# Cross-attention with a token branch on one core: unit maxima two or three a step, score halves issued singly, tile scores spread over the weighting phases

## The reference

```python
query = x @ Wq;  keyt = enc @ Wk;  valt = enc @ Wv      # enc: the first 150 context rows
hs = mha(query, keyt, valt)                             # 8 heads of 80, softmax over 150 keys
ca_q1 = einsum('btc,th->bch', ca, Wq_ca)                # 384 rows of rank 4
ca_q1 = ca_q1[:, linspace(0, 383, 2048), :]             # 384 rows repeated to 2048
ca_hs1 = mha(ca_q1, x, x)                               # softmax over the 2048 rows of x
ca_hs2 = mha(ca_hs1 @ Wq, ca @ Wk_ca, ca @ Wv_ca)       # softmax over 4 tokens
out = (hs + ca_hs2) @ Wout + b_out + x
```

## Time and profile before

| | |
|---|---|
| time of three runs | 1560.33, 1560.63, 1563.39 us; median 1560.63 |
| the profiled execution | 1563.7 us, of which the span is 1561.6 us |
| granted TensorE clock, mean | 0.994 |
| busy share PE, PEld, DVE, ACT | 97%, 80%, 51%, 40% |
| weighting phases of the batches, first exponential of the first phase to that of the second | 34.1, 33.2, 34.2, 33.1 us |
| second phase, to the end of its last exponential | 26.7 us in each batch |
| from there to the split of tile 1's output (ACT, line 1090) | 22.2 us in each batch |

### The profile page before, as it was taken

The page is one execution under the profiler, slowest core; times in us unless marked ns, Lnnn a source line. Parts: engine busy times, 40 slices in busy tenths (PEclk is TensorE's granted clock), DMA queues, the critical chain, the costliest instruction groups (busy, mean ns, idle before and its releaser), DMA issues.

```text
span 1561.6 us, 24534 instructions
## 1 busy us (share of the span) xinstructions
PE 1511.6 (97%) x10294; PEld 1245.7 (80%) x10294; DVE 791.3 (51%) x1595; ACT 617.7 (40%) x1310; POOL 2.8 (0%) x12
## 2 busy tenths in 40 slices
PE   5999999999999999999999999999999999999998
PEld 4763599999976379999997438999998744999998
DVE  5786335343467443543447826344345872443533
ACT  1427724233243853323333484223323367332322
POOL 0000000000000000000000000000000000000000
PEclk9999999999999999999999999999999999999999
DMA  6630012130253001122025200114004510021101
GB/s 233 212 131 33 1 38 84 49 118 26 93 173 118 1 6 57 65 86 77 35 105 184 86 1 20 55 53 154 18 34 154 176 37 1 19 93 57 60 18 42
DMA packets 46679, 117.26 MB, mean 75 GB/s; under 512 B 3661, under 2 KB 5317, under 8 KB 45019
## 3 DMA queue, kind: packets, MB, share of 16 engines
q1 hardware_dynamic: 37036, 93.91, 17.3%
q10 hardware_dynamic: 9535, 21.80, 3.6%
HBM read 77.33 MB, written 39.17 MB: 75 GB/s over the span
## 4 chain that ended last, share of the span: by engine, by line
PE 85%; DVE 7%; ACT 5%; issue 3%; DMA 0%; SPq 0%; ACTq 0%
PE ps_w L502 43%; PE ps_s L502 17%; PE ps_t L502 15%; PE ps_t L512 5%; DVE unit_max L1290 4%; ACT work L1107 4%; PE ps_w L512 3%; PE ps_s L512 1%; ACT work L1077 1%; ACT ot L1021 0%; DMA y_all<-in_L_xattn_Wv_ca_dram 0%; DVE xt_l L1375 0%; DVE neg_max L1344 0%; DVE ot L1405 0%; ACT ot L1090 0%
## 5 line engine op out<-in xcount | busy, mean ns | idle before, releaser
L502 PE MATMUL ps_w<-wo_h,ot 128*128 128x320 f32 x1280 | 310.4, 314 | 0.6 <-DVE ot L1405 0.6
L1290 DVE TENSOR_REDUCE unit_max<-ps_s 128x1 f32<-128x512 f32 x384 | 240.1, 684 | 51.3 <-PE ps_s L502 50.2
L1077 ACT ACTIVATE work<-ps_s,neg_max 128x150 f32<-128x150 f32 x512 | 155.6, 409 | 211.7 <-DVE neg_max L1348 211.7
L502 PEld LDWEIGHTS ps_w<-wo_h,ot 128*128 128x128 f32 x1280 | 220.3, 188 | 0.9 <-DVE ot L1405 0.9
L502 PE MATMUL ps_w<-wo_l,ot 128*128 128x320 f32 x640 | 197.4, 308 | 0.0
L502 PE MATMUL ps_w<-v_all,work 120*128 120x162 f32 (+1 forms) x1280 | 171.3, 288 | 1.9 <-ACT work L1072 1.9
L502 PEld LDWEIGHTS ps_w<-v_all,work 120*128 120x128 f32 x1280 | 170.3, 190 | 3.4 <-ACT work L1072 2.9
L502 PE MATMUL ps_s<-keys_h,qt_h 128*128 128x300 f32 (+1 forms) x448 | 138.1, 308 | 0.0
L502 PE MATMUL ps_s<-keys_h,qt_l 128*128 128x300 f32 (+1 forms) x448 | 131.5, 294 | 0.0
L502 PE MATMUL ps_s<-keys_l,qt_h 128*128 128x300 f32 (+1 forms) x448 | 131.0, 292 | 0.0
L1416 DVE TENSOR_TENSOR work<-ps_w,xc 128x320 f32<-128x320 f32 x128 | 62.5, 489 | 133.6 <-PE ps_w L502 133.6
(11 more groups left out here) (163 smaller groups left out, 2258.1 us busy)
## 6 DMA issues: line engine op xcount, KB each, us to landing
xc<-in_x_dram SPq DMA_DIRECT2D x32, 1280.0 KB, 6.6
out_dram<-work ACTq DMA_DIRECT2D x64, 320.0 KB, 2.2
xt_all<-work SPq DMA_DIRECT2D x60, 256.0 KB, 2.5
xt_l<-xt_all SPq DMA_DIRECT2D x12, 1280.0 KB, 5.6
y_all<-in_L_xattn_Wk_dram SPq DMA_DIRECT2D x4, 960.0 KB
y_all<-in_L_xattn_Wv_dram SPq DMA_DIRECT2D x4, 960.0 KB
pick<-pick_all SPq DMA_DIRECT2D x16, 194.0 KB
xc<-in_L_xattn_Wq_dram SPq DMA_DIRECT2D x1, 1600.0 KB, 10.7
```

The source lines that it names most:

```text
L502: return nc.tensor.matmul(out, lhs, rhs, start=start, stop=stop, skip_group_check=True)
L1077: return nc.scalar.activation(probs[:, h * KEYS:(h + 1) * KEYS], ps_s[:, bank, c * KEYS:(c + 1) * KEYS], exp, bias=neg_max[:, s % 2, h:h + ...
L1290: v.tensor_reduce(unit_max[:, a, n, q:q + 1], bank, AX_X, ALU.max).then_inc(max_free, 1)
```

## The change

The edits are all in the order of work, in these parts:

1. In the first phase the 34 units left (two stand before it) came three a step in steps 0 to 10 and one in step 11, behind both halves of the scores. Now `UNITS_STEP` gives 3 or 2 a step for steps 0 to 13: one ahead of the first half of the next step's scores, the rest between the halves. The scores of the second phase's first step are issued in step 15 before the last weigh; they followed it before.
2. `tile_scores` can be called for single runs. Tile 0's seven runs stand one or two a step from step 14 of the first phase to step 3 of the second (before: bank 0 in step 12, bank 1 in step 13, bank 2 behind the first phase). Tile 1's runs stand in steps 10 to 14 of the second phase (before: all behind it). `turn_ca(1)` stands in step 14 instead of 13.
3. Tile 0's exponentials stand in steps 6 to 13 of the second phase instead of 1 to 8, with a new semaphore `e0_done` after heads 2 and 5. `turn_z(0)` stands in step 8 instead of 10.
4. `turn_weights(0)` stands before the last weigh of the second phase instead of behind tile 1's scores; `turn_z(1)` stands behind `values(0)`; the copy of the second sums stands behind tile 0's two copies on ScalarE.
5. VectorE: `head_means(1)` and the first five operations of `shares` stand behind `normalise(0)`, and `output_low(0)` behind those, ahead of the rest of `shares`. `maximum(2)` goes from tile 0 behind `picked(0)` in tile 1; the two `x_low` of tile 0 go to tile 1, behind `add_rows(0, 0)`. ScalarE takes the output of tile 0 before the exponential of `s2`.
6. Three matmuls whose result nobody reads (128x512, into bank 2 of `ps_w`) stand before the first weigh of the first phase in each batch.

The numbers of matmuls of every kind are the same but for those three a batch.

```diff
-UNITS_STEP = 3
+UNITS_STEP = [3, 2, 3, 2, 3, 2, 2, 3, 2, 3, 2, 3, 2, 2, 0, 0]
+UNREAD_SUMS = 3
+RUNS_IN = {(0, 14): ((0, 0),), (0, 15): ((0, 1),), (1, 0): ((0, 2),), (1, 1): ((0, 3),), (1, 2): ((0, 4),), (1, 3): ((0, 5), (0, 6)),
+           (1, 10): ((1, 0),), (1, 11): ((1, 1), (1, 2)), (1, 12): ((1, 3), (1, 4)), (1, 13): ((1, 5),), (1, 14): ((1, 6),)}
+TURN_CA1, TURN_Z0, FIRST_EXP = 14, 8, 6
...
                     if st == 0 and a == 0:
                         pe.wait_ge(y_ones, 2 * (b + 1))
                         pe.wait_ge(q0_free, (b + 1) * KT)
+                        for n in range(UNREAD_SUMS):
+                            mm(ps_w[:, 2, :], wq_h[:, n, 0:P], xt_h[:, n, :], True, True)
...
                 for st in range(NST):
-                    if st + 1 < NST:
-                        scores(0, st + 1)
-                    units = min(UNITS_STEP, PHASES * UNITS - first)
-                    max_units(first, units)
-                    first += units
+                    a_next, st_next = divmod(st + 1, NST)
+                    ahead = UNITS_STEP[st] // 2
+                    max_units(first, ahead)
+                    scores(a_next, st_next, (0,))
+                    max_units(first + ahead, UNITS_STEP[st] - ahead)
+                    first += UNITS_STEP[st]
+                    scores(a_next, st_next, (1,))
                     weigh(0, st)
-                    if st == 12:
-                        tile_scores(0, (0,))
-                    if st == 13:
+                    if st == TURN_CA1:
                         turn_ca(1)
-                        tile_scores(0, (1,))
-                scores(1, 0)
-                tile_scores(0, (2,))
+                    for s, n in RUNS_IN.get((0, st), ()):
+                        tile_scores(s, (n,))
                 for st in range(NST):
                     if st + 1 < NST:
                         scores(1, st + 1)
+                    else:
+                        turn_weights(0)
                     weigh(1, st)
-                    if st == 10:
+                    if st == TURN_Z0:
                         turn_z(0)
-                tile_scores(1, (0,))
-                turn_z(1)
-                tile_scores(1, (1, 2))
+                    for s, n in RUNS_IN.get((1, st), ()):
+                        tile_scores(s, (n,))
...
                     values(s)
                     if s == 0:
-                        tile_scores(2, (0,))
+                        turn_z(1)
+                        tile_scores(2, (0, 1))
                         turn_o(0)
-                        tile_scores(2, (1, 2))
+                        tile_scores(2, (2, 3, 4, 5, 6))
...
                     if s == 1:
                         picked(0)
-                    if 1 < s < SLOTS - 1:
+                    if s and s < SLOTS - 1:
                         maximum(s + 1)
...
-                        output_low(0)
-                        maximum(2)
-                    if c + 1 < CHUNKS:
-                        for kt in X_AT[t]:
+                    if s == 1:
+                        add_rows(0, 0)
+                    if c + 1 < CHUNKS and s:
+                        for kt in X_AT[0] + X_AT[1] if s == 1 else X_AT[t]:
                             x_low(c + 1, kt)
-                    if s:
+                    if s > 1:
                         add_rows(s - 1, 0)
```

More of the change, by code:

```diff
@@ L729, in turn_ca, with scores @@
                     last.then_inc(ca_full, 1)
-                def scores(a, st):
-                    if st == 0:
+                def scores(a, st, halves=(0, 1)):
+                    if st == 0 and halves[0] == 0:
                         pe.wait_ge(ca_ready, b * PHASES + a + 1)
@@ L737, in scores @@
                             pe.wait_ge(g_ready, CHUNKS * (b + 1))
-                    for p in range(2):
+                    for p in halves:
                         k = (a * NST + st) * 2 + p
@@ L815, in tile_scores @@
                                    keys_h[:, at:at + hs, :].rearrange("p h k -> p (h k)"),
-                                   keys_l[:, at:at + hs, :].rearrange("p h k -> p (h k)"), bank != seen, True)
-                        seen = bank
-                    if banks[-1] == 2:
+                                   keys_l[:, at:at + hs, :].rearrange("p h k -> p (h k)"), first, True)
+                    if runs[-1] == ALL_RUNS[-1]:
                         last.then_inc(s_full, 1)
@@ L1108, in _ @@
                                                  scale=SCALE).then_inc(w_ready, 1)
[L1109 to L1110 removed]
+                        h = st - FIRST_EXP
+                        if a and 0 <= h < HEADS:
+                            if h == 0:
                                 act.wait_ge(nmax_ready, tile0 + 1)
[L1112 to L1113 removed]
+                            last = weight(0, h)
+                            if h == HEADS - 1:
                                 last.then_inc(p_ready, 1)
[L1115 to L1116 removed]
+                            elif h == BANK_HEADS[h // 3][-1]:
+                                last.then_inc(e0_done, 1)
                 def queries_next(s):
@@ L1125, in _ @@
                     remaining_weights(s)
+                    if s == 0:
+                        act.wait_ge(w_used, (b + 1) * PHASES * NST)
+                        nc.scalar.activation(ssum[:, :], sums, copy).then_inc(ssum_ready, 1)
                     if queries_next(s):
@@ L1450, in _ @@
                     if s == 0:
+                        head_means(1)
+                        zs.close()
+                        shares.done(v.tensor_tensor(s2_diff[:, 0, :, :], s2_diff[:, 0, :, :], s2_diff[:, 1, :, :], ALU.add))
+                        shares.done(v.tensor_reduce(s2_max[:, :], diffs, AX_X, ALU.max))
+                        shares.done(v.tensor_scalar(s2_max[:, :], s2_max[:, :], 0.0, None, ALU.max))
+                        v.tensor_scalar(by_head(s2)[:, :, 0], s2_max[:, :], -1.0, None, ALU.mult)
+                        v.tensor_tensor(by_head(s2)[:, :, 1:TOK], diffs, spread_t[:, :, 0:DIFF], ALU.subtract).then_inc(s2_ready, 1)
+                        output_low(0)
                         dve.wait_ge(e2_ready, b + 1)
```

52 lines of the change are left out of this document (25 added, 27 removed).

## The result

The changed kernel takes 1541.03 us (median of 4 runs, 1539.51 to 1541.37) against 1562.01 (4 runs, 1560.33 to 1563.79): ratio 0.9859, 95% interval 0.9846 to 0.9871. Its profiled execution took 1540.79 us, span 1539.0, against 1563.7 and 1561.6. The forecast was 1540.4, or 1543.5 for the profiled execution. The ratios in this document leave out two executions at a much lower granted clock, one of the kernel before (2355.99 us at 0.553) and one of the kernel with the two small waits (1649.57 us at 0.846).

A forecast was written before the change was run, and what follows sets the result against it. TensorE sets the end almost everywhere, VectorE the first phase's steps. -3.3 + 2.1 - 3.6 = -4.8 us a batch, -19.2 in four, and -1 for the clock: profiled 1563.7 to 1543.5, median 1540.4, range 1529 to 1552.

The forecast's parts named there:

- First phase, steps 0 to 13: 34 units spread over 14 steps: 25.0 us a batch, between bounds of 22.4 and 27.4.
- the conflict: First phase: a unit sharing a row group with the scores half delays it, making steps 1.81 or 2.09 us, not 1.48.
- VectorE idle in each step: Sign for first phase, steps 0 to 13: steps near 1.8 us, with VectorE idle in every one.
- Steps 14 and 15: End of the first phase: 4.1 us against 5.6, including 0.45 us of new wait for VectorE's copy.
- Second phase: Tile 0's and tile 1's runs add 4.0 us of TensorE work; the phase grows by 2.1 us a batch.
- half its time counts: Second phase: a run lies on one of two interleaved loops, so 2.0 of 4.0 us added count.
- Tail: From the last exponential into tile 1: 3.6 us a batch shorter, 3.1 to tile 1's start and 0.5 within it.
- less side by side: Rival, chance 0.13: units and neighbouring halves hold each other up, first-phase steps stay at 1.96 us; 1552.
- slower: Rival, chance 0.06: first-phase units waiting for banks starve ScalarE, over 2.13 us a step; 1582 if nothing overlaps.
- Everything overlaps: Rival, chance 0.12: the 14 first-phase steps take 1.60 us each, 22.4 us in all; 1530.
- Runs on the path in full: Rival, chance 0.09: all the time of the second phase's added runs counts, +2.0 us a batch; 1548.
- two interleaved loops: Loops of exponentials, scores and weigh, 3.2 us each, run beside each other one step apart: 1.60 us a step.

The follow-up runs named there:

- the kernel with the two small waits: Changed kernel with tile 0's second run moved to step 14 and tile 2's third ahead of `turn_o(0)`: 1540.05 us, and 1541.77 when timed again.
- three-behind kernel: Changed kernel with the 34 units three a step in steps 0 to 10, one in step 11, behind both score halves: 1553.16 us.
- combined: Changed kernel with no unit ahead of the first scores half, no unread matmuls, and two runs moved one place each against waits: 1534.48 us.
- lumped kernel: The combined kernel with tile 0's runs 1 to 6 in one lump behind the first phase's last weigh: 1535.95 us.
- run 3: No follow-up kernel: one of tile 0's seven runs of tile scores, counted from 0, standing in step 1 of the second phase; 0.61 us to the next scores.

## Why the prediction was right, and where its steps were off

The time was right within 1 us and the change of the profiled execution within 2.7 (-20.2 against -22.9). That it came so close is in part luck: the first phase was forecast 1.2 us a batch too long and the second 0.9 too short, and the two errors cancel but for 1.2 us in four batches.

- *First phase, steps 0 to 13*: 24.2 us with the unread matmuls, forecast 25.0 + 0.7. The gain of spreading and that of the place between the halves are each shown by a kernel of their own. The kernel without the unread matmuls has 23.44, which is 1.6 under the 25.0, and shows where. By the starts of ScalarE's exponentials, its six steps with a shared row group take 10.3 us, forecast 11.7; the eight others 13.1, forecast 12.8; and the 0.5 us for a short step behind a long one was not needed. So the term that was off most is the conflict: I let a shared row group delay the whole half (1.81 and 2.09 us a step), and in the rows above it delays one matmul of two by 0.34 us. The sign "VectorE idle in each step" did not come: twelve maxima stand in one piece.
- *Steps 14 and 15*: 4.4, forecast 4.1, although the wait for `ca_mat` was 0.23 and not 0.45. That the new order is the gain there is read from the three-behind kernel against the kernel before with the unread matmuls: 31.43 against 33.75, with steps 13 to 15 at 6.2 us instead of 8.5.
- *Unread matmuls*: +0.75 a batch, forecast +0.7. *Clock*: one stretch was expected to go, both went.
- *Second phase*: +3.0, forecast +2.1. The step that failed is the term "half its time counts", 0.6 for tile 0's runs and 1.4 for tile 1's. Tile 1's came near it (1.46). Tile 0's did not: steps 1 to 4 are 7.97 us against 6.61 before, that is +1.57 for the runs and -0.2 for tile exponentials that moved away. Half of the 0.76 us of runs that had stood at the start of the phase was taken off, and nothing came back for them: step 0 is 1.77 us with two runs before it, with one and with none (the three kernels before, changed and combined). The remaining 0.15 is the turn of the sums and the exponentials in steps 5 to 9. Why 1.57 and 1.46, see below.
- *Tail*: -3.68, forecast -3.6, the `turn_o` wait 0.37 against 0.4, the hole gone as said. (The 0.36 us for `turn_z(1)` is not the pace of `turn_o`'s five transposes, which gives 0.42, but it is what four take in the kernel before, 1318.63 to 1318.99.) To the start of tile 1 it is -2.96 (forecast -3.1), behind it -0.72 (-0.5). But without the moved copy the tail would be 2.2 us longer, not 0.5.
- *Rivals*: "less side by side" and "slower" are excluded by 1.73 us a step, against 1.96 and over 2.13. "Everything overlaps" is excluded as a time (1530), but not far off in the first phase: 23.44 us in the kernel without the unread matmuls is 1.0 from its 22.4 and 1.6 from the forecast's 25.0. "Runs on the path in full" had +2.0 a batch over the forecast, and 0.9 came.

**Which runs count.** The idea of two interleaved loops was right, and it gives both numbers if each loop is followed by itself. One loop of the changed kernel, from the exponentials of step 1 to those of step 3:

```profile
1270.05 0.83 ACT L1124 ACTIVATE work<-ps_w 128x768 f32<-128x768 f32 x1
1270.75 0.84 ACT L1124 ACTIVATE work<-ps_t 128x768 f32<-128x768 f32 x1
1271.64 0.44 PE L508 MATMUL ps_t<-ca_mat,ot 32*128 32x384 f32 x2
1272.00 0.85 PE L508 MATMUL ps_w<-work,y_all 128*32 128x384 f32 x8
1272.79 0.41 PE L508 MATMUL ps_s<-keys_h,qt_h 128*128 128x300 f32 x1
1273.03 0.30 PE L508 MATMUL ps_s<-keys_l,qt_h 128*128 128x300 f32 x1
...
1273.40 0.44 PE L508 MATMUL ps_w<-ca_mat,ot 32*128 32x384 f32 x2
1273.88 0.81 ACT L1124 ACTIVATE work<-ps_w 128x768 f32<-128x768 f32 x1 [0.29 <-PE ps_w L508]
```

The second exponential of step 1 ends at 1271.59. Behind it come the second half of step 2's scores, the weigh of step 1, the run of step 1, and the scores of step 3. So a run of step 1 delays step 3 and not step 2: runs of odd steps lie on one loop, runs of even steps on the other, and a loop spans two steps. Without runs two steps take 3.20 us (lumped kernel). To that each loop adds its own runs, at the time from their first matmul to the next scores. For the loop with the more work:

| steps | runs on the loop, us | 3.20 and that | measured |
|---|---|---|---|
| 1 and 2 | run 3, 0.61 | 3.81 | 3.83 |
| 3 and 4 | runs 5 and 6, 0.94 | 4.14 | 4.13 |
| 10 and 11 | tile 1's run 0, 0.61 | 3.81 | 3.81 |
| 12 and 13 | tile 1's runs 3 and 4, 1.04 | 4.24 | 4.26 |

The first two rows add 1.55 us, where 1.57 was measured. The last two add 1.65, less 0.2 because ScalarE's tile exponentials already make two steps 3.30 there (kernel with tile 1's runs behind): 1.45, where 1.46 was measured. The runs on the other loop fit under it. This account is read from the rows and from those two kernels; no kernel moves a run from one loop to the other, which would test it.

A run that stands alone takes 0.61 us and not the 0.42 of the forecast. Its second matmul starts 0.24 us after its first instead of 0.14, and the scores 0.23 after its last. The forecast had only the second of these: "nothing on the way in" misreads the kernel before, where the same 0.24 us stand behind a weigh (1283.08 to 1283.32). Over runs 2 to 6 it is 0.18 us for each of the four groups (2.65 us in the combined kernel, 1.94 by the prices of matmuls). Two of tile 0's groups and two of tile 1's lie on the loops of the table, so 0.7 of the 3.0 us a batch are the price of standing alone. The Trainium skill's rule that the forecast weighed (TensorEngine Tiling (Array Packing), Key Properties: a change of tiling mode drains TensorE) goes with this, and it was set too low at 0.09 us a group. That the mode is the cause isn't shown: 0.24 us also stand between the first two matmuls of a run behind `values`, whose matmuls are 120 rows deep (1325.35 to 1325.59 in the kernel before).

## What to carry to other kernels

Where two loops run beside each other, one step apart, work put into every step falls on them by turns. Add up each loop by itself: the one with the more work sets the time, and the work on the other is hidden. Price a small group by the time from its start to the start of what follows, not by its matmuls. A hole's length is not its worth: one of 0.23 us was worth nothing when a run of 0.42 was moved into it, and the edit behind one of 0.62 us was worth 2.2 once the work ahead of it was gone. Small groups cost least between the two halves here (first phase 28.05 us), more when some stand ahead of both (28.59), and most behind both (29.69).

## What the runs showed of the hardware

The preparation carries stretches of low clock whose number differs between executions, in batches whose instructions are the same. Batch 2 and batch 1 of the changed kernel, at the same place of the preparation:

```profile
845.00:849.00 4.00, 3.90 (x22) 2.53 (x20) 3.75 (x7) 0.60 (x1) 0.00 (x0) 1.00 0.52 137
849.00:853.00 4.00, 4.00 (x15) 3.41 (x15) 2.43 (x6) 0.98 (x2) 0.00 (x0) 0.57 0.90 320
...
470.10:474.10 4.00, 3.90 (x23) 2.57 (x23) 3.42 (x7) 0.60 (x1) 0.00 (x0) 1.00 0.22 76
474.10:478.10 4.00, 4.00 (x21) 2.95 (x21) 3.21 (x7) 0.98 (x2) 0.00 (x0) 1.00 0.96 308
```

```profile
849.11 1.58 PE L508 MATMUL ps_w<-gyw_b,work 128*128 128x56 f32 x8
...
475.79 1.10 PE L508 MATMUL ps_w<-gyw_b,work 128*128 128x56 f32 x8
```

With the clock at 0.57 (1.2 GHz for most of it, 2.4 for the rest), eight matmuls take 1.58 us instead of 1.10, and the preparation of batch 2 is 85.4 us long where that of batch 1 is 83.8. TensorE was 3.90 of 4 us busy ahead of the fall, and 3.90 ahead of the undisturbed stretch. The preparations of the profiled executions have none to four such stretches, about 1.6 us each, the kernel before one and the changed one also one. A difference of 2 to 3 us between two of these kernels has to be read from the stretches that the edit touches; why the clock falls in one batch and not in the next stays open.
